# Two-layer transformer kernel: one step per item for the layers behind, biases in the open bank, all low halves of the probabilities on GpSimd

## What is computed

```python
x = _layernorm(x + _L0_attn_ref(x, ...))   # 16 heads of 64, causal softmax, then @ Wo + bo
x = _layernorm(x + _L0_ffn_ref(x, ...))    # ternary weights round(W/gamma) in {-1,0,1}; relu(x W1^T + b1) W2^T + b2
x = _layernorm(x + _L1_attn_ref(x, ...))   # quantised attention, 16 heads of 4, then proj_w, + proj_b
x = _layernorm(x + _L1_ffn_ref(x, ...))    # 16 experts, top 1, capacity 128, gate = max of the softmax
```

## Time and profile before

| | us |
|---|---|
| median of 3 runs | 976.37 (975.16 to 976.71) |
| the profiled execution | 978.94 |
| its span | 976.9 |
| first low half on VectorE to the last normalisation (about 691 to 843) | 152 |
| last normalisation to the end of `check` (843 to 902) | 58 |
| end of `check` to the experts' first transposes (902 to 914) | 12 |
| experts, load back, last norm, store (914 to 977) | 63 |

### The profile page before, as it was taken

The page is one execution under the profiler, slowest core; times in us unless marked ns, Lnnn a source line. Parts: engine busy times, 40 slices in busy tenths (PEclk is TensorE's granted clock), DMA queues, the critical chain, the costliest instruction groups (busy, mean ns, idle before and its releaser), DMA issues. The chain is left out here.

```text
span 976.9 us, 26051 instructions
## 1 busy us (share of the span) xinstructions
PE 797.9 (82%) x10837; PEld 523.2 (54%) x10837; DVE 639.5 (65%) x1421; ACT 639.6 (65%) x847; POOL 635.8 (65%) x393
## 2 busy tenths in 40 slices
PE   5789999999999999999999999998865858632570
PEld 2344555666566666656566666665643645521570
DVE  5687778666776766767666676758839672646016
ACT  4347768788888887887888878887554526020342
POOL 6246777879888888888888888888443336131150
PEclk9789999999999999999999999999977765665695
DMA  6122138231231213023220412323100000430342
GB/s 172 39 45 45 28 83 183 50 73 24 50 81 37 45 33 85 17 58 74 46 45 19 93 24 45 73 60 67 18 1 1 12 12 7 132 106 8 98 148 83
DMA packets 91855, 56.72 MB, mean 58 GB/s; under 512 B 40394, under 2 KB 88136, under 8 KB 91606
## 3 DMA queue, kind: packets, MB, share of 16 engines
q1 hardware_dynamic: 89990, 52.00, 22.7%
q0 software_dynamic: 1024, 1.45, 0.5%
q10 hardware_dynamic: 720, 1.57, 0.4%
HBM read 16.64 MB, written 5.26 MB: 22 GB/s over the span
## 5 line engine op out<-in xcount | busy, mean ns | idle before, releaser
L1444 POOL TENSOR_TENSOR prob_lo<-prob,prob_hi 128x896 f16<-128x896 f32 (+2 forms) x310 | 565.5, 1843 | 186.4 <-ACT prob L1023 157.7
L1136 DVE TENSOR_REDUCE part_max<-psum 128x2 f32<-128x1024 f32 (+1 forms) x320 | 333.3, 1059 | 86.5 <-PE psum L729 66.6
L1020 ACT ACTIVATE prob_hi<-psum 128x1024 f16<-128x1024 f32 (+1 forms) x320 | 288.6, 902 | 143.4 <-PE psum L777 139.2
L1023 ACT ACTIVATE prob<-psum 128x1024 f32<-128x1024 f32 (+1 forms) x320 | 288.2, 900 | 0.0
L774 PE MATMUL psum<-high 128*128 128x512 f16 (+3 forms) x640 | 230.1, 360 | 47.8 <-ACT prob L1023 19.5
L800 PE MATMUL psum<-v,prob_hi 128*128 128x65 f16 x2176 | 238.6, 196 | 0.7 <-issue 0.7
L802 PE MATMUL psum<-v,prob_hi 128*128 128x64 f16 x2176 | 236.8, 194 | 0.5 <-issue 0.5
L804 PE MATMUL psum<-v,prob_lo 128*128 128x65 f16 x2176 | 236.8, 196 | 0.0
L777 PE MATMUL psum<-mixed 65*128 65x512 f16 (+3 forms) x640 | 226.4, 358 | 0.0
L800 PEld LDWEIGHTS psum<-v,prob_hi 128*128 128x128 f16 x2176 | 203.1, 99 | 37.5 <-issue 18.6
L802 PEld LDWEIGHTS psum<-v,prob_hi 128*128 128x128 f16 x2176 | 204.2, 99 | 15.1 <-issue 2.0
(11 more groups left out here) (210 smaller groups left out, 960.7 us busy)
## 6 DMA issues: line engine op xcount, KB each, us to landing
high<-kq SPq DMA_DIRECT2D x128, 128.0 KB
mixed<-kq SPq DMA_DIRECT2D x64, 128.0 KB
ew<-in_L_ffn_W SPq DMA_DIRECT2D x32, 256.0 KB
expert_rows<-zero SPq DMA_DIRECT2D x1, 1032.0 KB, 10.0
xe<-expert_rows SPq DMA_DIRECT2D x4, 258.0 KB, 4.2
prob<-in_L_attn_x SPq DMA_DIRECT2D x4, 256.0 KB, 6.3
mixed<-shift SPq DMA_DIRECT2D x64, 1.0 KB
expert_out<-zero SPq DMA_DIRECT2D x1, 1024.0 KB, 12.0
```

What stands on the lines that cost most here:

```text
L1020: act.activation(m.prob_hi[i % HI_RING][:, 0:u.width], src, ACT.Exp, scale=EXP_SCALE)
L1023: act.activation(m.prob[i % PROB_RING][:, 0:u.width], src, ACT.Exp, scale=EXP_SCALE)\
L1136: last = dve.tensor_reduce(m.part_max[:, g % 2, :, r, c:c + 1], src[:, :, col:col + width], AX, ALU.max)
L1444: pool.tensor_tensor(m.prob_lo[i % LOW_RING][:, c], m.prob[i % PROB_RING][:, c], m.prob_hi[i % HI_RING][:, c], ALU.subtract).then_inc(low_ ...
```

## The change

The tables place every item of every group by hand, separately for each engine (`PE_AT`, `ACT_AT`, `DVE_AT`, `POOL_AT`; `ONCE_AT` for what is done once). The layers behind get all eight banks from step 322 on (before that banks 4 and 5 only), the least recently used free one each time. The down projection is in four parts, one per slice. The biases `bo`, `b1`, `b2` are split into three bfloat16 rows on VectorE (steps 60 and 100, three small DMAs) and enter each bank as a first matmul with 3 rows. Every low half of the probabilities is made on GpSimd. The first norm is scaled on ScalarE; the transposes of x1 and x2 are float32, four in the place of eight; the split into halves comes after them, the high half on ScalarE and the low on VectorE. One relu per slice is left on ScalarE, and VectorE makes the low half out of PSUM. The third norm takes its input from r and `rstd` directly; x2 itself is made on GpSimd (`second`), and its transposes, only needed for the span, come late. The scaling of the third norm moves to ScalarE. The square root has 2 operations in the place of 4 ahead of its two iterations, in scalar_tensor_tensor form. `Wo`, `W1`, `W2` are loaded at step 280. The load of `xe` moves into the experts' block, one wait for each group. At the very end the square root is taken once for all 16 tiles, and ScalarE and VectorE scale 8 tiles each.

```diff
+SUMS = {"project": 2, "down": UPS - 1}
+PE_STAGES = (("project", 0), ("project", 1), ("project", 2), ("turn", 0), ("up", 0), ("up", 1), ("up", 2), ("up", 3),
+             ("down", 0), ("down", 1), ("down", 2), ("down", 3), ("turn3", 0), ("gate", 0), ("count", 0), ("turn", 1), ("span", 0))
+ACT_STAGES = (("norm", 0), ("turn", 0), ("up", 0), ("up", 1), ("up", 2), ("up", 3), ("third", 0), ("turn3", 0), ("turn", 1))
+DVE_STAGES = (("norm", 0), ("turn_low", 0), ("up", 0), ("up", 1), ("up", 2), ("up", 3), ("norm", 1),
+              ("gate", 0), ("count", 0), ("span", 0))
+POOL_STAGES = (("second", 0), ("scatter", 0))
+PE_AT = ((292, 294, 296, 298, 299, 301, 302, 303, 304, 304, 305, 305, 318, 318, 322, 353, 353), (297, 300, 301, 306, 308, 308, 310, 311, 312, 312, 313, 313, 323, 328, 330, 343, 355), (307, 314, 317, 319, 321, 322, 323, 324, 325, 325, 326, 328, 333, 339, 349, 343, 354), (328, 329, 329, 329, 335, 336, 336, 338, 336, 338, 341, 341, 372, 374, 384, 373, 379))
+ACT_AT = ((298, 299, 300, 302, 303, 305, 313, 319, 351), (306, 307, 309, 310, 311, 312, 325, 328, 347), (321, 323, 325, 326, 329, 330, 332, 339, 352), (331, 332, 334, 337, 341, 344, 355, 366, 386))
+DVE_AT = ((290, 297, 299, 300, 303, 304, 307, 317, 324, 353), (301, 307, 307, 308, 309, 310, 311, 330, 338, 356), (316, 317, 320, 323, 326, 326, 332, 342, 352, 364), (332, 333, 333, 334, 340, 340, 342, 376, 396, 379))
+POOL_AT = ((313, 369), (332, 390), (368, 408), (386, 414))
+ONCE_AT = (289, 288, 292, 290, 296, 298, 308, 320, 329, 333, 359, 360, 288, 396)
...
+            name = what, g, 0 if what in SUMS else part
+            if name not in fills:
+                bank = next(b for b in order if b not in kept and (i >= NU + LATE or b in (4, 5)))
+                order.remove(bank)
+                order.append(bank)
+                fills[name] = Fill(bank, made[bank])
+                made[bank] += 1
...
-    c.mark(dve.tensor_scalar(v, variance, EPS, None, ALU.add))
-    c.step(dve.tensor_scalar(half, variance, EPS, 0.5, ALU.add, ALU.mult))
-    c.step(dve.tensor_scalar(s.bitcast(I32), v.bitcast(I32), 1, None, ALU.logical_shift_right))
-    c.step(dve.tensor_scalar(s.bitcast(I32), s.bitcast(I32), ROOT_BITS, None, ALU.add))
+def one_over_deviation(dve, c, t, out, variance, n=4):
+    half, s, q = (work[:, 0:n] for work in t.work)
+    half_eps, bits = (t.root[:, k, 0:n] for k in range(2))
+    c.step(dve.scalar_tensor_tensor(half, variance, 0.5, half_eps, ALU.mult, ALU.add))
+    c.step(dve.scalar_tensor_tensor(s.bitcast(I32), half.bitcast(I32), 0.5, bits, ALU.mult, ALU.add))
     for _ in range(2):
         c.step(dve.reciprocal(q, s))
         c.step(dve.tensor_tensor(q, q, half, ALU.mult))
...
-def statistics(dve, c, t, x):
...
+def statistics(dve, c, t, x, n, g, off_ready=None):
...
-    one_over_deviation(dve, c, t.rstd[:], t.mv[:, :, 1], t.work)
...
+    one_over_deviation(dve, c, t, t.rstd[:, n, s], t.mv[:, n, s, 1])
+    last = dve.scalar_tensor_tensor(t.off[:, n, s], t.mv[:, n, s, 0], -1.0, t.rstd[:, n, s], ALU.mult, ALU.mult)
...
+                elif fill.bank < 6:
+                    b = fill.bank // 2
+                    pe.wait_ge(free[b], GIVEN[b])
...
+                    pe.wait_ge(acc_free, UNITS[-1].turn + 1 - (UNITS[-1].turn - fill.bank) % 2)
...
+                    pe.matmul(out, t.onesb[0:3, :], t.bias3[:, FF:FF + D].unsqueeze(1).broadcast_to([3, 4, D]),
+                              start=True, stop=False, skip_group_check=True)
...
-            def turn_halves(g, n):
-                pe.wait_ge(t.x_split[n], g + 1)
+            def turn(g, n):
+                pe.wait_ge(t.x2_ready if n else t.x1_ready[g], g + 1 if n else 1)
                 fill = start("turn", g, n)
-                for a, x in enumerate((t.x_hi[n], t.x_lo[n])):
-                    for k in range(4):
...
+                for k in range(4):
+                    x = t.x[:, 4 * g + k, :] if n else t.x1[g][:, k, :]
+                    last = pe.transpose(bank(fill)[:, k * P:(k + 1) * P], x, m.ident[:])
                 last.then_inc(t.tail_full[fill.bank], 1)
...
-            def down(g):
-                pe.wait_ge(t.up_lo_done, (g + 1) * FT)
-                fill = start("down", g)
+                out, c = bank(fill), slice(f * P, (f + 1) * P)
+                pe.matmul(out, t.bias3[:, c], t.onesb[0:3, :].unsqueeze(1).broadcast_to([3, 4, P]), start=True, stop=False)
...
+                else:
+                    pe.matmul(out, t.w1t[:, c], t.x1t[g % 2][:, 0, :], start=False, stop=False)
+                    last = pe.matmul(out, t.w1t[:, c], t.x1t[g % 2][:, 1, :], start=False, stop=True)
+                last.then_inc(t.tail_full[fill.bank], 1)
...
+            def down(g, f):
+                fill = FILLS["down", g, 0]
...
+                wait_free(pe, "up", g, f)
...
-                act.activation(t.up_hi[g][:, f, :], bank(fill), ACT.Relu, bias=m.ffn_b1[:, f:f + 1])
-                if g > 0:
-                    act.wait_ge(t.up_lo_done, (g - 1) * FT + f + 1)
-                elif f == 0:
...
-                act.activation(t.up[:, f, :], bank(fill), ACT.Relu, bias=m.ffn_b1[:, f:f + 1])\
-                    .then_inc(t.tail_free[fill.bank], 1)
...
+                else:
+                    act.activation(t.up_hi[g][:, f, :], bank(fill), ACT.Relu).then_inc(t.up_high, 1)
...
+            def scale(g, n):
+                act.wait_ge(t.off_ready, OFFS.index((g, n)) + 1)
...
+                    j = 4 * g + k
+                    x = t.x3[g][:, k, 0:D] if n else t.x1[g][:, k, :]
+                    last = act.activation(x, x if n else t.r[g][:, k, :], ACT.Identity, scale=t.rstd[:, n, j:j + 1],
+                                          bias=t.off[:, n, j:j + 1])
+                last.then_inc(t.x3_ready[g] if n else t.x1_ready[g], 1)
...
+            def place_low(g):
+                fill = FILLS["turn", g, 0]
+                x = t.x1t[g % 2]
+                dve.wait_ge(t.x1_high, g + 1)
+                dve.tensor_tensor(x[:, 1, :], bank(fill), x[:, 0, :], ALU.subtract).then_inc(t.tail_free[fill.bank], 1)
+            def up(g, f):
+                fill = FILLS["up", g, f]
+                hi, lo = t.up_hi[g][:, f, :], t.up_lo[g][:, f, :]
+                dve.wait_ge(t.up_high, FT * g + f + 1)
+                dve.scalar_tensor_tensor(lo, bank(fill), 0.0, hi, ALU.max, ALU.subtract).then_inc(t.tail_free[fill.bank], 1)
...
+            def third(g):
...
                 for k in range(4):
-                    last = normal(dve, t, x[:, k, :], t.r, k)
+                    last = dve.scalar_tensor_tensor(x[:, k, :], t.r[g][:, k, :], t.rstd[:, 1, 4 * g + k:4 * g + k + 1],
+                                                    t.pb_b[:], ALU.mult, ALU.add)
...
-                dve.wait_ge(t.x_ready[n], g + 1)
-                c.step(dve.tensor_copy(t.x_hi[n][:], x))
-                dve.tensor_tensor(t.x_lo[n][:], x, t.x_hi[n][:], ALU.subtract).then_inc(t.x_split[n], 1)
...
+            def make_low(u):
                 i = u.index
                 pool.wait_ge(free[u.buf], u.turns + 1)
...
                 pool.tensor_tensor(m.prob_lo[i % LOW_RING][:, c], m.prob[i % PROB_RING][:, c], m.prob_hi[i % HI_RING][:, c],
-                                   ALU.subtract).then_inc(low_pool, 1)
...
-            def bias(g):
...
+            def second(g):
+                pool.wait_ge(t.mean_ready, g + 1)
+                for k in range(4):
+                    last = pool.tensor_scalar(t.x[:, 4 * g + k, :], t.r[g][:, k, :], t.mv[:, 1, 4 * g + k, 0:1],
+                                              t.rstd[:, 1, 4 * g + k:4 * g + k + 1], ALU.subtract, ALU.mult)
+                last.then_inc(t.x2_ready, 1)
...
+            def load_weights():
+                scored(HEADS - 3)
+                sp.dma_start(m.wo[:], ins["L0_attn_Wo"].rearrange("(a p) n -> p a n", p=P)).then_inc(t.late_w, 16)
+                sp.dma_start(m.ffn_w1[:], ins["L0_ffn_W1"].rearrange("(a p) n -> p a n", p=P)).then_inc(t.late_w, 16)
+                sp.dma_start(m.ffn_w2[:], ins["L0_ffn_W2"]).then_inc(t.late_w, 16)
...
+            sp.wait_ge(t.scattered, 16 * TILES)
+            for b in range(GROUPS):
+                src = t.rows_in[4 * b * P:(4 * b + 4) * P, :].rearrange("(e c) d -> c e d", c=P)
+                sp.dma_start(t.xe[:, tiles(b), :], src).then_inc(t.xe_in[b], 16)
...
+            act.wait_ge(last_scale, 1)
             for g in range(GROUPS):
-                act.wait_ge(last_scale, g + 1)
-                for k in range(4 * g, 4 * g + 4):
+                for k in range(4 * g, 4 * g + 2):
...
-                c.wait()
-                one_over_deviation(dve, c, rstd[:, tiles(g)], mv[:, tiles(g), 1], t.work)
-                dve.scalar_tensor_tensor(shift[:, tiles(g)], mv[:, tiles(g), 0], -1.0, rstd[:, tiles(g)], ALU.mult,
-                                         ALU.mult).then_inc(last_scale, 1)
+            c.wait()
```

(9 more changed lines are left out.)

451 lines of the change are left out of this document (211 added, 240 removed).

## The result

The changed kernel takes 926.06 us (median of four runs, 924.85 to 927.77) where the kernel before took 976.54 beside it: a ratio of 0.9486, with a 95% interval of 0.9467 to 0.9504. It is 50 us faster. The forecast was 915 us in a range of 896 to 945; the sign and the range hold, and the forecast is 11 us too low. The profiled execution has a span of 923.0 us.

What follows compares the result with a forecast made beforehand. From 690 us on it took the order of the work, not a full engine, as the limit. Span 976.9 - 52.7 (to `check`'s end) - 3 (handover) - 5.3 (end) = 915.9; median forecast 915 us, range 896 to 945.

Steps and rivals of the forecast that it cites:

- PE's work: PE from the 704 us mark to the last weighting: 57.3 us at full clock, against 67 before.
- 704 + 57 + 9 + 4 = 774: Last normalisation's end: start mark, PE's work, waits and lower clock; with 8 us of contention the forecast was 782.
- I take 1.1 us for each, half a low half: 8 us: Delay to VectorE's statistics chains, units 290 to 319, from meeting GpSimd's subtractions; bounds 0 and 45 us.
- The seven chains: VectorE's chains of statistics between units 290 and 319, while GpSimd subtracts 57 of some 78 us; each priced at 1.1 us.
- small operations average over 0.4 us: Test that would show the forecast wrong: VectorE's small square-root operations, expected at 0.16 to 0.18 us, averaging above this.
- A blocked one per chain at most: Expected sign in the square root: no more than one small VectorE operation held up in each chain of statistics.
- the contention rival: Each of seven VectorE chains meets two more 2.13 us GpSimd subtractions, 30 us on PE's path: 945 us; chance 0.16.
- the bound of 45 us: Upper bound for contention between VectorE and GpSimd: 2.13 us three times a chain.
- None above 3: PE's waits from 704 us to the last weighting: together 9 us, each at most 3, so the clock mostly keeps its upper level.
- 67 us instead of 58.5: Last normalisation to the end of `check`: VectorE about 50, holes 14, contention 3; bounds 58 and 76.
- a gain of 3: Handover from `check` to the experts, load of `xe` behind the block change: about 12.5 against 15.7 us; bounds 0 and 5.
- The end, 5.3: Final square root and scalings: roots save 7 us, ScalarE's scaling takes 3.3 instead of 1.65; gain bounds 3 and 6.5.

Runs made afterwards that it cites:

- e9: Changed kernel with GpSimd making only the first 128 columns of the low halves of items 307 to 319, the rest left out: 916.75 us, ratio 0.9395.
- e1: Changed kernel with the four-column inverse square root and its shift using only VectorE instructions with one tensor operand from SBUF: 950.58 us, ratio 0.9754.
- e5: Changed kernel with the load of the experts' rows back in the first block, ahead of the change of blocks: 928.31 us, ratio 0.9507.
- e6: e1 plus group 0's third transpose and gate and group 2's first transpose moved behind item 318's weighting, against the changed kernel: 953.69 us, ratio 0.976.
- e17: Changed kernel with GpSimd's second norm of group 0 behind the last low half, and VectorE making the low halves of items 315 and 317: 922.55 us, ratio 0.9454.
- e18: As e17, with the low half of item 308 also made by VectorE, ahead of group 0's third term: 921.92 us, ratio 0.9447.
- b2: Kernel before with only the new end: one root over 16 columns and half of the scalings on VectorE: 971.7 us, ratio 0.9955.
- b1: Kernel before with only all low halves of the probabilities moved to GpSimd: 982.73 us, ratio 1.0061.
- e3: Changed kernel with GpSimd's second norm of group 0 moved behind the last low half: 924.32 us, ratio 0.9466.

## Why the prediction was right, and where it was not

**PE's work and the waits for exponentials: right.** The stage was read as a stage of waits in which the order decides, and the new order took 52.8 us from it (843.2 to 790.4); the sum had 61.2. PE's waits for exponentials fell from 18.5 to 1.2 us. PE's work was right: 65.38 us busy at a clock of 0.86 is 56 at full clock, against 57. With the low halves cut (e9) the last normalisation ends at 776.8; the prediction's terms without contention give 704 + 57 + 9 + 4 = 774. That sum was right to 3 us, though e9 still has 2.7 us of excess on VectorE in it.

**"I take 1.1 us for each, half a low half: 8 us": mis-sized.** This is the step that failed. The excess on VectorE was 16.5 us, and its effect on the last normalisation 13.6 (e9), on the whole 9. The prediction stayed near the low end "since before a chain met one subtraction at most". That row belongs to an order in which GpSimd was often idle when a root ran. In the new order ScalarE delivers six items in a row while VectorE runs the longest chain, so nearly all two-operand instructions of one chain meet the same burst. The seven chains were not alike: one lost 9.6 us, one 5.5, and the other five together about 1.4. A rate over the stage could not show that; walking the two engines' orders side by side for the last units might have.

One of the two rows behind the step was also misread. The operation of 1.74 us at 705.97 (L526 in the earlier trace rows) reads one tensor of four columns and not two. It said already that four columns and one operand can be blocked, which e1 then met.

The test named for the step, "small operations average over 0.4 us", fired for the root's product and sum (0.70 and 0.43); over all nine operations of a root the mean is 0.36, so the test was worded too loosely. "A blocked one per chain at most" failed plainly: one chain had five of them in the root and the shift. The result lies between the forecast and the contention rival (945), which had the right cause and, like the forecast, the wrong count.

The Trainium skill, "SBUF — State Buffer", section "SBUF: two separate sides", was cited beside that step for a lock on shared ports that is held for the whole instruction, and by it the third term would be near its upper bound. The trace agrees with the mechanism (1.6 to 2.2 us for a 0.16 us instruction) and with the direction of that remark. It does not reach the bound of 45 us: the chains left the run of low halves when it ended, and that run was 11.1 us long for the longer chain and three single low halves for the other.

**"None above 3": wrong.** Two waits of 6.5 and 10.5 us, with the granted clock at 0.55 and 0.54 around and behind them; its mean over the stage is 0.86 and not the 0.9 asked for. Both waits are the same step again: with the low halves cut they are 1.7 and 1.5.

**"67 us instead of 58.5": 5 too many.** It took 61.7. Of the terms, VectorE's work was 46.8 us instead of 50 and the holes 15 instead of 14 and 3 for contention. Part of this is not a better forecast but a transfer: when PE waits in the stage before, VectorE is at work on what comes later (this reason is argued, the size is measured). With the waits away (e9) the stretch took 66.3, next to the forecast, and 4.5 of the 13.6 us gained before it were given back. The two stages were priced as if they were independent.

**Handover, "a gain of 3": wrong.** It gained 0.1. The change of blocks was taken as 5.4 us from the median landing. In the new place SyncE issues the load 7.0 us after the last scatter (853.08 to 860.10), another 3.1 pass to the first transposes and 4.5 to the first product. So the change of blocks and the transfer still stand in a row, and the new place is worth e5's 1.3 us. The rest goes with a path that the forecast left out. It had GpSimd's last four scatters beside `check`; in fact twelve scatters, of groups 1 to 3, stand in one row on GpSimd from 836.27 us on and end at 853.08, 0.9 us behind `check`. In e1, e6, e17 and e18 they end 0.2 to 0.8 us ahead of it, and there the handover takes 13.3 to 13.8 us, near the 12.5 of the forecast.

**The end, 5.3: right to 1 us.** Alone it measures 4.4 (b2).

**Both signs in one edit.** All low halves on GpSimd was counted as 12 us off VectorE against 8 of contention. Alone, in the old order, it costs 6 us (b1). In the changed kernel it was not undone as a whole, so what it costs or brings there is not known. Two or three of them back at chosen places (e17, e18), together with e3's move, give medians 3.5 and 4.1 us lower; against e3 alone it is 1.8 and 2.4, which the intervals do not part from nothing.

**The 11 us added up.** 7.1 lie in the span by the terms above: 8.4 at the last normalisation, 5.3 back, 3 at the handover, 1 behind the first product. The other 4 are no mechanism: the profiled execution was the quickest of the four, with a span 3.1 us under the median of the times, where the prediction had put the median 0.9 us under the span.

Whether a second open bank earlier than step 322 would help was not tried: the other buffers are still the attention's there. Nor was a root with its scratch in PSUM, since the free columns share banks with PE's running sums.

## What to carry to other kernels

Work that leaves a busy engine for its neighbour is only cheaper if the two do not meet in a shared resource. Lay the timelines of both side by side at the place of the longest chain and count how long the neighbour's run without a gap is: here a chain of small dependent instructions that entered such a run left it when the run ended (14.5 to 14.9 us in three kernels). Making the chain shorter or longer, or changing which of its instructions is blocked, then gave little; shortening the run (e9) brought 9 us.

When a chain of dependent small instructions sets the end, count instructions, not only their width: four one-column instructions cost more than three times one of four columns, and 2.1 us more in each of twelve roots went with 24.5 us of time.

When work is deferred, follow it on every engine to the place where the next stage waits for all of them: twelve scatters that nobody had put in the sum set the start of the handover.

## What the runs showed of the hardware

- A block is not only a matter of two operands. In e1 the first instruction of the root, one tensor operand of four float32 columns, took 1.50 us from 739.01, to the end of GpSimd's low half (738.35 to 740.48), and 0.17 when none ran; the one-column instructions were never held up, inside bursts or outside. The Trainium skill, "VectorE: DVE Perf Modes", section "What auto-detection actually checks", names a two-port mode for a single source and a destination in SBUF whose outermost non-unit dimensions are both even or equal. The four-column instruction fits that; why the one-column ones stayed free no run here shows.
- VectorE's reciprocals on four columns, one operand too, took 0.18 us inside every burst.
- GpSimd's instruction with one tensor operand (the second norm, 0.79 us each) hardly blocks: beside it VectorE's small instructions, of one operand and of two, took 0.16 to 0.39 us (e1 and the changed kernel).
- GpSimd's second norm took 3.13 us for four 128x128 tiles where the prediction had 1.6; moving it away gained nothing clear of the noise (e3).
